# Attention and expert kernel on one core: x rows normalised on GpSimd, x part of the logits scaled on ScalarE

## What is computed

```python
x = x + cross_attention(layernorm(x), ctx_768)   # x: 32 x 100 x 256, ctx: 32 x 361 x 192
x = x + ffn(layernorm(x))

# cross attention: both sides are normalised once more, with gains and offsets
q = x1 @ Wq + bq;  k = x2 @ Wk + bk;  v = x2 @ Wv + bv
attn = softmax(q k^T * 256**-0.5);   out = (attn @ v) @ Wo + bo

# ffn: one shared expert, 31 routed ones, the top 3 of which each token takes
shared = gelu(x @ ws1 + bs1) @ ws2 + bs2
aff = softmax(x @ Wr + br);  vals, idx = top_k(aff, 3)
routed = sum over the three of vals * (gelu(x @ We1[e] + Be1[e]) @ We2[e] + Be2[e])
return shared + routed + x
```

## Time and profile before

| | us |
|---|---|
| median of three runs | 493.3 |
| the three runs | 494.15, 491.27, 493.30 |
| the profiled execution | 494.56 |
| its span, first to last instruction | 492.9 |
| mean granted TensorE clock in it, of full speed | 0.984 |
| busy in the span: TensorE, VectorE, ScalarE, GpSimd | 461.0, 357.1, 253.7, 308.7 |

### The profile page before, as it was taken

The page is one execution under the profiler, slowest core; times in us unless marked ns, Lnnn a source line. Parts: engine busy times, 40 slices in busy tenths (PEclk is TensorE's granted clock), DMA queues, the critical chain, the costliest instruction groups (busy, mean ns, idle before and its releaser), DMA issues.

```text
span 492.9 us, 13620 instructions
## 1 busy us (share of the span) xinstructions
PE 461.0 (94%) x3168; PEld 400.0 (81%) x3168; DVE 357.1 (72%) x1614; ACT 253.7 (51%) x848; POOL 308.7 (63%) x316
## 2 busy tenths in 40 slices
PE   8899979999999998879999999999999999999991
PEld 8677757777777877668999898899999999999891
DVE  4958879999999997773567666666666666661784
ACT  1455747676767667462445454445554555543220
POOL 3312385858585857671588888788888888884000
PEclk9999999999999999989999999999999999999997
DMA  7555668877578944893599999898888888875999
GB/s 241 150 172 151 219 208 255 274 239 257 189 235 286 334 149 154 276 360 105 116 184 187 185 183 181 157 145 138 136 137 137 139 135 138 136 107 101 350 348 322
DMA packets 81151, 97.54 MB, mean 198 GB/s; under 512 B 9201, under 2 KB 65906, under 8 KB 81074
## 3 DMA queue, kind: packets, MB, share of 16 engines
q1 hardware_dynamic: 60786, 70.79, 46.9%
q0 software_dynamic: 19248, 25.40, 30.8%
q10 hardware_dynamic: 1040, 0.48, 0.5%
HBM read 54.91 MB, written 41.73 MB: 196 GB/s over the span
## 4 chain that ended last, share of the span: by engine, by line
PE 50%; DVE 15%; issue 10%; DMA 10%; SPq 5%; POOL 3%; ACT 2%; POOLq 0%; DVEq 0%; ACTq 0%
PE bank L1271 12%; PE bank L1282 12%; DMA sum<-y_sb,token 6%; PE bank L1260 3%; PE bank L1106 2%; PE bank L1107 2%; PE bank L1118 2%; DVE w_all L792 2%; PE bank L1158 2%; DMA xt<-expert_rows_in 2%; POOL sum L579 2%; DVE c L741 2%; DMA w_all<-sum 2%; PE bank L1186 2%; PE bank L1159 2%
## 5 line engine op out<-in xcount | busy, mean ns | idle before, releaser
L579 POOL DMA_INDIRECT sum<-y_sb,token x105 | 170.8, 1626 | 48.0 <-issue 24.1
L689 ACT ACTIVATE up<-bank,b_all 128x128 f32<-128x128 f32 x260 | 81.4, 364 | 102.2 <-PE bank L1271 66.1
L1271 PE MATMUL bank<-xtt,w1b 128*128 128x128 f32 x840 | 111.4, 276 | 0.3 <-ACT xtt L715 0.3
L1282 PE MATMUL bank<-w_all,up 128*128 x420 | 108.8, 382 | 0.1
L1271 PEld LDWEIGHTS bank<-xtt,w1b 128*128 128x128 f32 x840 | 102.1, 192 | 0.8 <-ACT xtt L715 0.5
L984 DVE TENSOR_SCALAR y_sb<-bank,gate,inverse 128x256 f32<-128x256 f32 x105 | 57.1, 544 | 55.4 <-PE bank L1282 54.7
L557 POOL DMA_INDIRECT expert_rows_in<-xt,slot x75 | 74.4, 992 | 24.6 <-issue 24.0
L1282 PEld LDWEIGHTS bank<-w_all,up 128*128 128x128 f32 x420 | 71.7, 191 | 6.1 <-issue 0.2
L976 DVE COPY w1b<-w_all 128x512 f32 x105 | 47.7, 454 | 18.1 <-PE bank L1271 7.5
L715 ACT ACTIVATE xtt<-bank 128x256 f32<-128x256 f32 x105 | 40.2, 384 | 39.3 <-PE bank L1260 38.7
L534 POOL TENSOR_TENSOR rs<-mv,eps_cols 128x5 f32<-128x5 f32 (+1 forms) x32 | 8.0, 252 | 62.2 <-DVE mv L849 62.0
(11 more groups left out here) (199 smaller groups left out, 883.4 us busy)
## 6 DMA issues: line engine op xcount, KB each, us to landing
xt<-expert_rows_in SPq DMA_DIRECT2D x105, 132.0 KB, 2.6
w_all<-in_w SPq DMA_DIRECT2D x47, 256.0 KB
w_all<-in_ctx SPq DMA_DIRECT2D x32, 288.0 KB, 3.1
w_all<-sum SPq DMA_DIRECT2D x15, 384.0 KB, 7.3
sum<-pad_rows SPq DMA_DIRECT2D x1, 3328.0 KB, 12.0
w_all<-in_x SPq DMA_DIRECT2D x25, 128.0 KB, 3.1
sum<-y_sb SPq DMA_DIRECT2D x25, 128.0 KB
sum<-xt SPq DMA_DIRECT2D x25, 128.0 KB
```

The costliest lines, as they stand in the source:

```text
L579: pool.indirect_dma_start(sums[s], bass.IndirectOffsetOnAxis(ap=token[sx][:, 0:1], axis=0), y_sb[sx][:, :], None, compute_op=ALU.add).then ...
L689: ins = act.activation(up[s][:, m * P:m * P + P], up_ps[s][:, m * P:m * P + P], ACT.Gelu, bias=b1_all[:, e, m:m + 1].rearrange("p o n -> p ...
L1271: mm = pe.matmul(up_ps[s][:, m * P:m * P + P], w[:, c * INTER + m * P:c * INTER + m * P + P], xtt[s][:, c * P:c * P + P], start=(c == 0), ...
L1282: mm = pe.matmul(down_ps[s], up[s][:, m * P:m * P + P], w, start=(m == 0), stop=(m == 1))
```

## The change

Two instructions move to other engines, with their semaphores.

GpSimd normalises the x tile. It does so in the step in which it makes the deviation, behind the power, for `starts(i + 2)`; VectorE did it one step later. It waits for its own power, and for TensorE to have transposed the tile before last out of the same buffer. VectorE's statistics of x now wait until GpSimd has read those of the tile before last.

ScalarE scales the x part of the tile that ended, as the first thing of its step. VectorE waits for it ahead of the reciprocal.

```diff
@@ GpSimd, step(i), behind the power
+                x = starts(i + 2)
+                if x is not None:
+                    pool.wait_ge(ctx_rstd, i + 3)
+                    if x >= 2:
+                        pool.wait_ge(x_transposed, x - 1)
+                    pool.tensor_scalar(z1[x % 2], x_sb[x % 8], mv[i % 2][:, 3, 0:1], rs[i % 2][:, 1, 3:4],
+                                       ALU.subtract, ALU.mult).then_inc(x_norm, 1)
@@ ScalarE, head of step(i)
+                t = ends(i - 3)
+                if t is not None:
+                    act.wait_ge(attn_made, t + 1)
+                    act.wait_ge(x_dev_made, t + 1)
+                    if t >= 2:
+                        act.wait_ge(parts_read, t - 1)
+                    act.activation(x_part[t % 2][:, :], attn_ps[:, RB:RB + NE], ACT.Copy,
+                                   scale=x_dev[:, t % 8:t % 8 + 1]).then_inc(x_part_made, 1)
@@ VectorE, step(i)
                     dve.wait_ge(attn_made, mixed + 1)
+                    dve.wait_ge(x_part_made, mixed + 1)
                     dve.reciprocal(rinv[m2][:, :], attn_ps[:, D1:D1 + 1]).then_inc(rinv_made, 1)
-                    dve.wait_ge(x_dev_made, mixed + 1)
-                    dve.tensor_scalar(x_part[m2][:, :], attn_ps[:, RB:RB + NE], x_dev[:, mixed % 8:mixed % 8 + 1], None,
-                                      ALU.mult).then_inc(x_part_made, 1)
...
-                    dve.wait_ge(x_part_made, mixed + 1)
                     dve.scalar_tensor_tensor(logit_part[m2][:, :], attn_ps[:, RA:RA + NE], rinv[m2][:, 0:1], x_part[m2][:, :],
                                              ALU.mult, ALU.add).then_inc(parts_read, 1)
...
-                if met_x is not None:
-                    s = met % 2
-                    if met_x >= 2:
-                        dve.wait_ge(x_transposed, met_x - 1)
-                    dve.tensor_scalar(z1[met_x % 2], x_sb[met_x % 8], mv[s][:, 3, 0:1], rs[s][:, 1, 3:4],
-                                      ALU.subtract, ALU.mult).then_inc(x_norm, 1)
...
                     if new_x is not None:
+                        if new_x >= 2:
+                            dve.wait_ge(x_norm, new_x - 1)
                         dve.bn_aggr(mv[n2][:, 3, :], x6[new_x % 2][:, :])
```

More of the change, by code:

```diff
@@ L735, in step @@
                 new, met, rated = batch(i + 2), batch(i + 1), batch(i - 1)
-                new_x, met_x = starts(i + 2), starts(i + 1)
+                new_x = starts(i + 2)
                 mixed, routed, ranked = ends(i - 3), ends(i - 4), ends(i - 5)
```

## The result

The changed kernel takes **500.31 us** (median, 498.11 to 500.89) where the kernel before took 493.51 beside it: ratio 1.0138, interval 1.0093 to 1.0183, slower by 6.8 us. The forecast was 491.1 us with a range up to 496.0, so it was wrong, and in its sign too. Ratios leave out executions in a slower state, which only a second chip showed (3 of 9 of e6, 6 of 11 of e7 and 8 of 27 of the kernel before there). The profiled execution took 499.86 us with a span of 497.7 (before: 494.56 and 492.9).

A forecast was written before the change was run, and what follows sets the result against it. TensorE and VectorE were taken as full together in the steady loop. Gains of 4.95 us less costs of 0.25, 1.0 and 1.5 us gave -2.2 us: 493.3 to 491.1 us, range 488.3 to 496.0.

The forecast's parts named there:

- The slot of the normalisation: GpSimd's time per moved normalisation, taken as 0.6 us from two-input adds; 0.25 us charged for it.
- The rule for a longer slot: Each 0.1 us beyond 0.6 costs up to 0.2 us in three four-step runs, 0.1 us in two three-step runs.
- rival (d): GpSimd becomes the loop's bound; a slot of 1.4 us adds 6.4 us, giving 497.5 us; chance 0.16.
- its deciding point of 0.9: Normalisation slot, about 0.9 us, from which rival (d) decides and the forecast gain is gone.
- Gains of 2 x 1.3 us at 135 and 187 us: In the attention loop, TensorE's two waits for VectorE's normalised x rows vanish, 1.3 us gained at each.
- 1.4 us from 58 to 84 us: Around the first scatters, TensorE's waits and the scatter start improve; 1.4 us gained, 2.4 us at most.
- the 12 us named as a sign: Sign of being right: VectorE's busy time down by some 12 us, with idleness in its place.
- The start, 0.65 us: Before TensorE's transpose at 22.39 us, two normalisations leave VectorE's row: 2 x 0.32 = 0.65 us gained.
- L1118 pushed by the x part, 1.0 us: Loop steps without ScalarE slack: x part delays copies TensorE needs, 4 x 0.2 + 2 x 0.1 = 1.0 us lost.
- The end, 1.5 us: Last tile's x part queues behind two Gelus on ScalarE, ending near 211.2 us; TensorE's L806 comes 1.5 us later.
- the longer idleness: At the loop's end, TensorE's longer idleness might prolong its lower clock, making the loss 2.5 us.
- Contention: GpSimd's add slowed beside VectorE's normalisation of h, 0.13 us a meeting, 25 meetings; covered by idle time, nothing charged.

The follow-up runs named there:

- e6: Kernel before plus one normalisation-form instruction on scratch on GpSimd ahead of its loop, second chip: ratio 0.9935.
- e7: Changed kernel, but GpSimd normalises only tiles 0 to 6, 9, 13, 16, 20, 23 and VectorE keeps all x parts; second chip: ratio 0.9920.
- e10: Kernel before plus 25 two-input adds of 256 columns on GpSimd and one scratch instruction ahead of its loop: 491.43 us.
- e9: Kernel before plus 25 unread normalisation-form instructions on GpSimd in its loop and one ahead of it: 501.34 us, ratio 1.0182.
- e12: Same kernel as e7, again on the first chip: 488.34 us, ratio 0.9909 to the kernel before.
- e2: Changed kernel with the normalisation back on VectorE, so only the x part moves to ScalarE: 495.62 us, ratio 1.0041.
- e4: As e2, but the last three x parts (tiles 22 to 24) stay on VectorE: 493.52 us, ratio 1.0023.
- e5: Kernel before with 16 empty instructions on GpSimd ahead of its loop, second chip: ratio 1.0065.
- e1: Changed kernel with the x part back on VectorE, so only the normalisation moves to GpSimd: 498.24 us, ratio 1.0101.
- e3: Changed kernel, but only tiles 0 to 6 normalised on GpSimd, later tiles and all x parts on VectorE: 490.42 us, ratio 0.9936.
- e11: Same kernel as e6, again on the first chip: 490.45 us, ratio 0.9944 to the kernel before.

## Why the prediction was wrong, point by point

- **The slot of the normalisation: this is the step that failed.** I took 0.6 us between bounds of 0.5 and 1.8, "as an add and a multiply are nearer to these adds than to a power". It is 1.2 us, and 1.3 us in the step's row, where it also waits about 0.1 us for the power. I measured nearness by the arithmetic. What counted is the form of the instruction, and of a tensor with two columns as scalars GpSimd had no row at all. With e10 the rest of the step is borne out: at a slot of 0.57 us the cost is as forecast (there with VectorE unrelieved). With e9, whose slot is 1.20 us, the loss of the loop is there in full.
- **The rule for a longer slot** was right in kind and too low: 0.73 us beyond 0.6 gives 3 x 1.46 + 2 x 0.73 = 5.8 us by rival (d); the loop lost 7.9. From e10 to e9 the slot grows by 0.63 us, for which the rule has 5.0 us, and the loop by 8.0. The four steps of the earlier trace rows grew by 3.87 us, where three slots of 1.3 us less the 0.54 us of idleness make 3.4. Rival (d), at 0.16, is what happened. Between my own bounds of 0.5 and 1.8 us its deciding point of 0.9 lay well inside, so it deserved nearer to a half; the range ought to have reached its 497.5 us, and even this falls short of the 500.31 measured.
- **Gains of 2 x 1.3 us at 135 and 187 us, and 1.4 us from 58 to 84 us**: they did not come. The waits went from VectorE's normalisation to GpSimd's (3.7 us in 4 places), and in the changed kernel the L1048 at 134.80 waits 0.76 us for L680 instead. Where GpSimd has time (e12) 0.5 us comes back at two of these waits and stays, for one L811 ahead of each; the prediction let two L811 and two L748 leave. VectorE's busy time fell by 6.7 us (357.1 to 350.4), not by the 12 us named as a sign.
- **The start, 0.65 us**: the wait of the earlier trace rows fell from 1.88 to 1.61 us, and the instruction starts at 22.05 instead of 22.39, 0.34 us earlier. All five kernels with the first tiles on GpSimd have this shorter wait.
- **L1118 pushed by the x part, 1.0 us**: over-sized. L622 took 0.28 us with a slot near 0.17, and the loop of e2 lost 0.2 us.
- **The end, 1.5 us**: right, 1.51 us at the instruction that was named, and 1.8 us at the first expert tile; e2 had 1.56 there, all at a clock of 0.90 as in before, so the longer idleness did not prolong the lower clock here. The last x part too ended where it was forecast: at 214.38 us, 12.5 us behind the last score product, where 211.2 is 12.6 behind that of before. It holds VectorE up by 3.6 us (12.58 less 8.95), of which the 2.01 us of idleness of the earlier trace rows took up the greater part.
- **The first use, 2.7 us**: in no case. The row at 58.29 us with its 3.88 us "<-issue" stood in the trace, and I passed over it as I had no name for it. It hid part of the loss: without it the change costs nearly 10 us.
- **Contention, charged at nothing**: this held. The add of 5 columns takes 0.33 to 0.34 us in nine steps of before, in all of which it starts 0.11 to 0.12 us behind VectorE's L855 (128x256, one tensor from SBUF, two columns as scalars) and has 0.5 us or more of idle time ahead of it, which covers the 0.13 us. It takes 0.21 us in the four steps in which it starts 0.34 us or more behind L855, though L859, which reads two tensors of 31 columns, runs beside it there.

## What to carry to other kernels

Price an instruction by a row of its own form on its engine, not by rows of similar arithmetic; where there is none, keep both bounds in the chances, and let the case that lies between them weigh accordingly. Work moved to an engine with idle time on average pays only in the steps that have the idle time: five of eighteen places took it for nothing, the others turned the engine into the bound. And an unexplained wait in front of a first instruction of its kind is worth one throwaway instruction earlier on, before any work is moved.

## What the runs showed of the hardware

- On GpSimd a `tensor_scalar` with two columns as scalars took 0.82 us for 128x32, 0.80 for 128x128 and 1.23 for 128x256; a two-input add of 128x256 0.64 us, a copy 0.40, a memset 0.31. VectorE's slot for the same normalisation was 0.32 us.
- GpSimd's first indirect scatter waited 2.5 to 4.2 us for nothing that the profile shows in the four kernels that had run no `tensor_scalar` on GpSimd (before, e2, e4, e5), and 0.18 us in the ten that had (after, e1, e3, and e6 to e12). Sixteen empty instructions in front of the loop did not help (e5). The Trainium skill, "GPSIMD Engine Reference", section 2.1, has a first call of a freshly loaded GpSimd routine pay about 6 us with no visible instruction. The trace agrees in kind with 2.3 to 4.1 us; the first `tensor_scalar` itself took no longer than later ones (1.23 us in e11 at 5.05 us, 1.22 in after at 131.74), so what the wait is, and how that instruction removes it, stays open.
- One chip ran the kernel before in 514.23 us, the other in 493.3. On the slower one ScalarE stood idle in the loop for reasons outside what the profile shows, as here in e6 (waits of 75 to 211 us; L666 is before's L664):

```profile
ACT tok L666 <- remote: 11.2, 5, 3.0
```

- TensorE's granted clock between 22 and 27 us had a mean of 0.66 to 0.67 in some executions, part of it at 0.50 (1.2 GHz), and 1.00 (2.4 GHz) in others, with the same kernel among both, on two chips (e11, e6). TensorE had stood idle 1.87 and 1.88 us just before in these two, so the idle time alone does not tell which it will be. The fall costs 1.6 to 3 us when it comes.
- From 197 to 232 us the mean clock was 0.90, 0.95 or 1.00 from one profiled execution to the next, and the same work, from the last score product to the first expert tile, took 34.5 to 34.9, 33.2 to 33.5 or 32.2 us.
- GpSimd's add of 128x5 took 0.21 us, and 0.33 to 0.34 us when it started within 0.12 us behind VectorE's `tensor_scalar` over 128x256.
